# FFN tail of a gated-experts kernel: tiles taken in pairs, the grid from the absolute value in one VectorE instruction, every subtraction on VectorE, GpSimd issues the stores alone

## What is computed

```python
def _quant_e4m3(t):
    amax = jnp.max(jnp.abs(t)).astype(jnp.float32)
    scale = jnp.maximum(amax / 448.0, 1e-12)
    return (t.astype(jnp.float32) / scale).astype(jnp.float8_e4m3fn), scale

def _L0_ffn_ref(x, weight):
    w_fp8, w_scale = _quant_e4m3(weight)
    x_fp8, x_scale = _quant_e4m3(x.reshape(-1, 512))
    acc = jnp.matmul(x_fp8.astype(jnp.float32), w_fp8.T.astype(jnp.float32))
    return (acc * (x_scale * w_scale)).astype(jnp.bfloat16)

x = x + jnp.tanh(g_xattn[0]) * _L0_xattn_ref(_layernorm(x), ids, ctx, ctx, ctx)
x = x + jnp.tanh(g_ffn[0]) * _L0_ffn_ref(_layernorm(x), L0_ffn_weight)
```

## Time and profile before

| what | us |
|---|---|
| median of 3 runs | 216.4 |
| the runs | 216.09, 216.40, 217.02 |
| span of the profiled execution, first to last instruction | 215.6 |
| busy in it: VectorE | 171.0 |
| busy in it: TensorE matmul | 157.5 |
| busy in it: ScalarE | 115.8 |
| busy in it: GpSimd | 102.2 |
| tail: from the end of `x_inv` to the end of the span | 161.5 to 215.6 |

### The profile page before, as it was taken

How to read it: one execution, slowest core, us unless ns; L and a number is a source line. 1 busy time by engine, 2 the same in 40 slices (tenths; PEclk the granted TensorE clock), 3 DMA queues, 4 the chain that set the end, 5 groups by cost and what they waited for, 6 DMA issues and landing times.

```text
span 215.6 us, 3505 instructions
## 1 busy us (share of the span) xinstructions
PE 157.5 (73%) x763; PEld 76.0 (35%) x764; DVE 171.0 (79%) x377; ACT 115.8 (54%) x185; POOL 102.2 (47%) x131
## 2 busy tenths in 40 slices
PE   0224967299999999999999999996711947485710
PEld 0102343044555455545555544543200412132300
DVE  2895799898746877888778688799678999999820
ACT  2565692466546765567656633723119786536410
POOL 6177888512334323434443322156112457978671
PEclk9999999579999999999999999999665596958785
DMA  3838996000000000000000000000000002322232
GB/s 48 332 109 221 390 373 189 0 0 2 0 3 0 2 0 0 0 0 0 0 0 0 3 0 0 3 0 0 2 0 0 0 24 87 120 111 93 105 157 87
DMA packets 5643, 13.25 MB, mean 61 GB/s; under 512 B 1024, under 2 KB 1536, under 8 KB 5632
## 3 DMA queue, kind: packets, MB, share of 16 engines
q0 software_dynamic: 2560, 8.39, 11.0%
q1 hardware_dynamic: 2784, 4.73, 6.4%
q10 hardware_dynamic: 288, 0.00, 0.1%
HBM read 8.92 MB, written 4.19 MB: 61 GB/s over the span
## 4 chain that ended last, share of the span: by engine, by line
PE 43%; DVE 25%; issue 14%; POOL 8%; ACT 5%; DMA 1%; DVEq 1%; POOLq 0%
PE y_ps L448 6%; PE y_ps L440 6%; PE y_ps L453 6%; PE a_ps L448 6%; PE a_ps L440 5%; PE a_ps L453 5%; PE zT_ps L480 3%; DVE w_bits L753 3%; DVE hT_lo L1019 3%; POOL out L330 3%; POOL x L307 3%; PE hT_ps L431 3%; DVE w_lo L800 2%; DVE x L1048 1%; ACT w_hi L582 1%
## 5 line engine op out<-in xcount | busy, mean ns | idle before, releaser
L338 POOL TENSOR_TENSOR z<-az,sg 128x512 f32<-128x512 f32 x15 | 19.1, 1271 | 30.0 <-ACT az L606 21.6
L325 POOL TENSOR_TENSOR rstd<-var,minus_half 128x1 f32<-128x1 f32 x16 | 11.1, 692 | 46.5 <-DVE var L864 46.5
L604 ACT ACTIVATE sg<-a_ps,job_inv_a 128x512 f32<-128x512 f32 x19 | 13.1, 687 | 23.3 <-PE a_ps L453 19.9
L440 PE MATMUL a_ps<-w_hi,hT_hi 128*128 x76 | 22.0, 404 | 4.2 <-ACT w_hi L582 4.1
L330 POOL DMA_INDIRECT out<-x,token_of x16 | 20.1, 1254 | 8.0 <-DVE x L1048 5.1
L850 DVE SCALAR_TENSOR_TENSOR x<-y_ps,job_mul,x 128x512 f32 x19 | 14.2, 748 | 8.4 <-PE y_ps L453 8.4
L440 PE MATMUL y_ps<-w_hi,zT_hi 128*128 x76 | 19.9, 384 | 1.4 <-DVE x L850 1.4
L307 POOL DMA_INDIRECT x<-in_x,token_of x16 | 17.4, 1089 | 7.0 <-issue 4.2
L448 PE MATMUL y_ps<-w_lo,zT_hi 128*128 x76 | 20.4, 392 | 0.0
L453 PE MATMUL y_ps<-w_hi,zT_lo 128*128 x76 | 20.1, 387 | 0.0
L613 ACT ACTIVATE zT_hi<-zT_ps 128x512 f16<-128x512 f32 x19 | 11.3, 594 | 16.3 <-PE zT_ps L480 16.3
(11 more groups left out here) (161 smaller groups left out, 338.4 us busy)
## 6 DMA issues: line engine op xcount, KB each, us to landing
w<-in_ctx_t SPq DMA_DIRECT2D x4, 1024.0 KB, 9.1
wf<-in_wf_t SPq DMA_DIRECT2D x1, 512.0 KB
x<-in_x,token_of POOLq DMA_INDIRECT x16, 3.6
out<-x,token_of POOLq DMA_INDIRECT x16
g_s<-in_g_x ACTq DMA_DIRECT2D x1, 0.5 KB, 2.7
ids_s<-in_ids SPq DMA_DIRECT2D x1, 8.0 KB, 2.5
g_s<-in_g_f ACTq DMA_DIRECT2D x1, 0.5 KB, 6.5
```

Source lines behind the costliest of these rows:

```text
L338: pool.tensor_tensor(z[:, :], az[:, :], sg[:, :], ALU.mult).then_inc(z_done, 1)
L440: pe.matmul(ps, lhs_hi(k), w_block(w_hi, expert, k), start=(k == 0), stop=False)
L604: act.activation(sg[:, :], a_ps[:, :], ACT.Silu, scale=job_inv_a[:, bass.ds(j, 1)]).then_inc(silu_done, 1)
```

## The change

Only the tail's code changes, and one allocation. What it does:

- The 16 tiles form 10 groups: tiles 0 and 1 alone, six pairs (2 and 3 up to 12 and 13), tiles 14 and 15 alone. Each instruction of VectorE and ScalarE handles a group: 512 or 1024 columns. TensorE has the same transposes and matmuls, with one wait and one signal for a group.
- `scaled` takes the absolute value on ScalarE. `exponents` is gone; `grid` is vm = max(|v|, 1.5 x 2^-6) times 2^20, from |v| itself.
- `rounded` is on VectorE for all tiles, directly behind `shifted` of the same group. GpSimd has 16 stores in a row and no arithmetic.
- `finish` runs two groups behind, `scaled` four groups ahead. The four matmul results are slices of one tensor `four_ps` of four banks, and the transposes of a pair share one bank of bfloat16.
- The rings keep their sizes in tiles; ve is dropped, and `q8_done` is one counter.

The diff, without the semaphore names and the comments:

```diff
         vt = w_hi[:, :].bitcast(F32)[:, 0:NB * D].rearrange("p (b d) -> p b d", b=NB)
-        v_ve = hT_lo[:, :].bitcast(BF16).rearrange("p (b d) -> p b d", d=D)
-        v, ve = v_ve[:, 0:NB, :], v_ve[:, NB:2 * NB, :]
+        v = hT_lo[:, :].bitcast(BF16).rearrange("p (b d) -> p b d", d=D)[:, 0:NB, :]
         vm_q8 = hT_hi[:, :].bitcast(BF16).rearrange("p (b d) -> p b d", d=D)
         vm, q8 = vm_q8[:, 0:NB, :], vm_q8[:, NB:2 * NB, :]
...
+        FIRST = [0, 1, 2, 4, 6, 8, 10, 12, 14, 15, TILES]
+        GROUPS = len(FIRST) - 1
...
-        a_ps = psum("a_ps", [P, D], F32)
-        y_ps = psum("y_ps", [P, D], F32)
-        hT_ps = psum("hT_ps", [P, D], F32)
-        zT_ps = psum("zT_ps", [P, D], F32)
+        four_ps = psum("four_ps", [P, 4 * D], F32)
+        a_ps, y_ps, hT_ps, zT_ps = [four_ps[:, n * D:(n + 1) * D] for n in range(4)]
...
-        STORE_LAG = 5
-        def on_pool(i):
-            return i % 4 != 0 and i < TILES - 1
+        def tiles_of(g):
+            return range(FIRST[g], FIRST[g + 1])
+        def ring(t, g, n):
+            first = FIRST[g] % n
+            return t[:, first:first + len(tiles_of(g)), :]
+        def rows_of(t, g):
+            return t[:, FIRST[g] * D:FIRST[g + 1] * D].rearrange("p (b d) -> p b d", d=D)
+        def through(tile):
+            return next(g for g in range(GROUPS) if tile in tiles_of(g)) + 1
+        def reused(g, n):
+            last = FIRST[g + 1] - 1 - n
+            return through(last) if last >= 0 else None
...
-                pool.wait_ge(out_done, i + 1)
+                pool.wait_ge(out_done, through(i))
...
             for i in range(TILES):
-                if on_pool(i):
-                    pool.wait_ge(vt_done, i + 1)
-                    if i >= NB:
-                        pool.wait_ge(qT_done, i - NB + 1)
-                    pool.tensor_tensor(q8[:, i % NB, :], vt[:, i % NB, :], vm[:, i % NB, :], ALU.subtract)\
-                        .then_inc(q8_done[i], 1)
-                if i >= STORE_LAG:
-                    store_tile(i - STORE_LAG)
-            for i in range(TILES - STORE_LAG, TILES):
                 store_tile(i)
...
-            def transpose_q(i):
-                pe.wait_ge(q8_done[i], 1)
-                if i >= NQ:
-                    pe.wait_ge(qT_copied, i - NQ + 1)
-                for k in range(K):
-                    mm = pe.transpose(qT_ps[i % NQ][:, k * P:(k + 1) * P], q8[:, i % NB, k * P:(k + 1) * P],
-                                      ident_bf[:, :])
+            def transpose_q(g):
+                pe.wait_ge(q8_done, g + 1)
+                if g >= NQ:
+                    pe.wait_ge(qT_copied, g - NQ + 1)
+                for n, i in enumerate(tiles_of(g)):
+                    for k in range(K):
+                        mm = pe.transpose(qT_ps[g % NQ][:, n * D + k * P:n * D + (k + 1) * P],
+                                          q8[:, i % NB, k * P:(k + 1) * P], ident_bf[:, :])
                 mm.then_inc(qT_done, 1)
 
             pe.wait_ge(pool_const, 13)
             pe.wait_ge(wfq_done, K // 2)
             pe.wait_ge(wfs_done, 1 + K // 2)
             transpose_q(0)
-            for i in range(TILES):
-                if i + 1 < TILES:
-                    transpose_q(i + 1)
-                pe.wait_ge(qT_copied, i + 1)
-                if i >= NF:
-                    pe.wait_ge(y8_done, i - NF + 1)
-                for k in range(K):
-                    mm = pe.matmul(f_ps[i % NF][:, :], qT[:, i % NF, k * P:(k + 1) * P], wf_q[:, k * D:(k + 1) * D],
-                                   start=(k == 0), stop=(k == K - 1))
+            for g in range(GROUPS):
+                if g + 1 < GROUPS:
+                    transpose_q(g + 1)
+                pe.wait_ge(qT_copied, g + 1)
+                if reused(g, 4):
+                    pe.wait_ge(y8_done, reused(g, 4))
+                for i in tiles_of(g):
+                    for k in range(K):
+                        mm = pe.matmul(four_ps[:, i % 4 * D:(i % 4 + 1) * D], qT[:, i % NF, k * P:(k + 1) * P],
+                                       wf_q[:, k * D:(k + 1) * D], start=(k == 0), stop=(k == K - 1))
                 mm.then_inc(f_done, 1)
...
-            def scaled(i):
-                if i >= NB:
-                    act.wait_ge(ve_done, i - NB + 1)
-                act.activation(v[:, i % NB, :], block_of(h2, i), ACT.Copy, scale=x_inv[:, :]).then_inc(v_done, 1)
-            def copy_qT(i):
-                act.wait_ge(qT_done, i + 1)
-                if i >= NF:
-                    act.wait_ge(f_done, i - NF + 1)
-                act.activation(qT[:, i % NF, :], qT_ps[i % NQ][:, 0:D], ACT.Copy).then_inc(qT_copied, 1)
-            def to_bf16(i):
-                act.wait_ge(f_done, i + 1)
-                if i >= NB:
-                    act.wait_ge(out_done, i - NB + 1)
-                act.activation(y8[:, i % NB, :], f_ps[i % NF][:, :], ACT.Copy, scale=out_scale[:, :])\
-                    .then_inc(y8_done, 1)
+            def scaled(g):
+                if reused(g, NB):
+                    act.wait_ge(vm_done, reused(g, NB))
+                act.activation(ring(v, g, NB), rows_of(h2, g), ACT.Abs, scale=x_inv[:, :]).then_inc(v_done, 1)
+            def copy_qT(g):
+                act.wait_ge(qT_done, g + 1)
+                if reused(g, NF):
+                    act.wait_ge(f_done, reused(g, NF))
+                n = len(tiles_of(g))
+                act.activation(ring(qT, g, NF), qT_ps[g % NQ][:, 0:n * D].rearrange("p (b d) -> p b d", d=D), ACT.Copy)\
+                    .then_inc(qT_copied, 1)
+            def to_bf16(g):
+                act.wait_ge(f_done, g + 1)
+                if reused(g, NB):
+                    act.wait_ge(out_done, reused(g, NB))
+                act.activation(ring(y8, g, NB), ring(four_ps[:, :].rearrange("p (b d) -> p b d", d=D), g, 4),
+                               ACT.Copy, scale=out_scale[:, :]).then_inc(y8_done, 1)
 
             act.wait_ge(xm_step, 5)
-            V_AHEAD, Y_BEHIND = 7, 1
-            for i in range(V_AHEAD):
-                scaled(i)
-            for i in range(TILES + Y_BEHIND):
-                if i < TILES:
-                    copy_qT(i)
-                if i + V_AHEAD < TILES:
-                    scaled(i + V_AHEAD)
-                if i >= Y_BEHIND:
-                    to_bf16(i - Y_BEHIND)
+            V_AHEAD, Y_BEHIND = 4, 1
+            for g in range(V_AHEAD):
+                scaled(g)
+            for g in range(GROUPS + Y_BEHIND):
+                if g < GROUPS:
+                    copy_qT(g)
+                if g + V_AHEAD < GROUPS:
+                    scaled(g + V_AHEAD)
+                if g >= Y_BEHIND:
+                    to_bf16(g - Y_BEHIND)
...
-            def exponents(i):
-                b = i % NB
-                dve.wait_ge(v_done, i + 1)
-                if i >= NB:
-                    dve.wait_ge(vm_done, i - NB + 1)
-                dve.tensor_scalar(ve[:, b, :].bitcast(I16), v[:, b, :].bitcast(I16), EXP_MASK >> 16, None,
-                                  ALU.bitwise_and).then_inc(ve_done, 1)
-            def grid(i):
-                b = i % NB
-                dve.wait_ge(ve_done, i + 1)
-                if i >= NB:
-                    dve.wait_ge(q8_done[i - NB], 1)
-                dve.tensor_scalar(vm[:, b, :], ve[:, b, :], 2.0 ** -6, 1.5 * 2.0 ** 20, ALU.max, ALU.mult)\
+            def grid(g):
+                dve.wait_ge(v_done, g + 1)
+                if reused(g, NB):
+                    dve.wait_ge(q8_done, reused(g, NB))
+                dve.tensor_scalar(ring(vm, g, NB), ring(v, g, NB), 1.5 * 2.0 ** -6, 2.0 ** 20, ALU.max, ALU.mult)\
                     .then_inc(vm_done, 1)
 
-            def shifted(i):
-                b = i % NB
-                dve.wait_ge(vm_done, i + 1)
-                dve.scalar_tensor_tensor(out=vt[:, b, :], in0=block_of(h2, i), scalar=x_inv[:, :], in1=vm[:, b, :],
-                                         op0=ALU.mult, op1=ALU.add).then_inc(vt_done, 1)
-            def rounded(i):
-                b = i % NB
-                dve.wait_ge(vt_done, i + 1)
-                if i >= NB:
-                    dve.wait_ge(qT_done, i - NB + 1)
-                dve.tensor_tensor(q8[:, b, :], vt[:, b, :], vm[:, b, :], ALU.subtract).then_inc(q8_done[i], 1)
-            def finish(i):
-                dve.wait_ge(y8_done, i + 1)
-                dve.scalar_tensor_tensor(out=block_of(x1, i), in0=y8[:, i % NB, :], scalar=tg[:, 1:2],
-                                         in1=block_of(x1, i), op0=ALU.mult, op1=ALU.add).then_inc(out_done, 1)
-            OUT_BEHIND = 5
-            exponents(0)
+            def shifted(g):
+                dve.wait_ge(vm_done, g + 1)
+                dve.scalar_tensor_tensor(out=ring(vt, g, NB), in0=rows_of(h2, g), scalar=x_inv[:, :],
+                                         in1=ring(vm, g, NB), op0=ALU.mult, op1=ALU.add).then_inc(vt_done, 1)
```

(29 more changed lines are left out.)

4 lines of the change are left out of this document (1 added, 3 removed).

## The result

| | kernel before | changed kernel |
|---|---|---|
| median of 4 runs | 216.71 us | 211.05 us |
| the runs | 216.09 to 217.16 | 208.60 to 211.72 |
| ratio, 95% interval | | 0.971 (0.967 to 0.975) |
| span of the profiled execution | 215.6 | 210.0 |
| VectorE busy in it | 171.0 | 160.4 |

The change makes the kernel 2.9% faster by the ratio. Forecast were 211.1 us and a range of 206.8 to 214.5.

The account below looks back on a forecast made before the run. VectorE was taken to bound the tail, with stores adding the end: floor 205.5 us, plus 2.6 for half clock, 1.8 for waits at the end, 0.4 for collisions, gave span 210.3; with 0.8 around it, 211.1 us, range 206.8 to 214.5.

Parts of the forecast that it names:

- VectorE bounds, and GpSimd's subtractions cost it most: Tail: VectorE has no idle time; 11 GpSimd subtractions cost it 10.0 us, 11 stores 1.7, of 11.7 lost.
- The sum up to the last pair's finish: VectorE's tail: 31.4 us of work from 162.28 plus 0.4 for ScalarE's second \|v\|, last pair finished near 194.2.
- Waits in the middle: Finishes of pairs wait for y8 at half clock, 0.87 us more per pair; 3 of 6 pairs, 2.6 us.
- half clock throughout: Rival: TensorE at 1.2 GHz through all pairs, 5.2 us in the middle, 3.5 at the end; 216.0 us, chance 0.07.
- Waits at the end: Single groups at the end shorten VectorE's period while the last pairs' chain stays long: 1.2 to 3.5 us, taken 1.8.
- Collisions of stores with VectorE: VectorE loses 0.15 us at each of 13 stores, most of it within waits: 0.4 us, bounds 0 and 2.0.
- Behind the last pair: Stores queued after the last pair's finish: 6.55 us, then 4.76 us to the span's end.
- What lies around the tail: Tail's first VectorE instruction at 162.28 as before; 0.8 us around the span, from median 216.4 against span 215.6.
- Full clock: Rival: TensorE at 2.4 GHz through the pairs, 2.6 us goes, 1.8 becomes 1.2; span 207.1, time 207.9 us, chance 0.19.
- Stores as the bound: Rival: every store meets a pair instruction in full, 2.54 us each; 216.4 us, no change, chance 0.07.
- Table loads: Rival: ScalarE's table lacks absolute value, so switching with Copy loads tables, 1.28 us each, 14 times; 222 us, chance 0.03.
- Grid at the plain rate: Rival: VectorE's grid instruction falls to its plain rate, 6.3 us more; 217.4 us, chance 0.04.

Follow-up runs that it names:

- filler kernel: Changed kernel plus unread TensorE matmuls into a free PSUM bank before the first transposes and where TensorE would pause: 208.74 us, ratio 0.962 to the kernel before.
- second profile: Profile from timing the changed kernel, unaltered, once more on another chip: 210.01 us, ratio 0.967 to the kernel before.
- the six: Six extra GpSimd subtractions into a buffer nobody reads, one per pair, added to the changed kernel: 216.19 us, ratio 0.995 to the kernel before.

## Why the prediction was right, and where its steps were not

**VectorE bounds, and GpSimd's subtractions cost it most: right.** Forecast was 10.0 us for the subtractions and 1.7 for the stores. The experiment with only the subtractions moved measured 11.3 and 0. The step that split 11.7 us between them was wrong, by taking the 0.91 of one subtraction for all eleven; it had no effect on the sum, in which all of it went, except for the collisions below.

**Durations of pairs: right.** Forecast for grid, shifted, rounded, finish: 0.42, 1.27, 1.21, 1.27; measured 0.42, 1.28, 1.22, 1.28. Slopes taken from instructions of 512 and 2048 columns held.

**The sum up to the last pair's finish: 0.6 us short.** 37.16 us lie between the first grid (161.54) and the end of the last pair's finish (198.70); 4.61 of them are waits for y8, which leaves 32.55 for the 31.9 between 162.28 and the 194.2 of the forecast. Each of the five waits also loses the 0.08 us by which instructions overlap, 0.4. Some 0.2 is spread over shifted and rounded.

**Waits in the middle: right mechanism, sized by luck.** 2.6 forecast; 0.34 + 1.82 + 0.48 + 1.19 = 3.8 measured in the first profile and 0.34 + 0.35 + 0.63 = 1.3 in the second. That the chain fits at full clock was right for pairs (no wait at three finishes in the filler kernel). Two terms were missing or mis-sized. A pair at half clock between pairs at full clock waits for most or all of the 1.7 us between chain and period (1.82 and 1.19 us measured), not for the 0.87 that was worked out for half clock throughout. And the first finish (0.34, at half clock) and the first pair's at full clock (0.35 and 0.36) wait where VectorE's period is shorter beside single tiles, which had no term. The even share of half and full clock was about right for the first profile (2 of 6 pairs at half clock and one mixed) and not for the second (one mixed). The finish three behind took all of these waits away.

**Waits at the end: too large.** 1.8 forecast, 0.78 measured on the path (0.80 in the second profile), with the last stretch at full clock throughout; at full clock throughout the forecast had 1.2. The 0.26 after it lies beside a queued store. The sign "over 0.5 us a group at full clock" is met only here, where the prediction itself had waits.

**Collisions of stores with VectorE: none.** 0.4 forecast (bounds 0 and 2.0), 0 measured. Stores are the ones that wait.

**Behind the last pair: right.** 6.55 forecast, 6.47 measured, then 4.83 against 4.76.

**What lies around the tail: two errors that cancel.** The tail began 0.74 us sooner than in the profile of before; the instruction that writes `x_inv` starts between 160.4 and 161.4 us in the profiles of all kernels here, and the changed code is not ahead of it. What lies around the span is 1.7 us (211.72 for the profiled run, span 210.0), not 0.8: the median of before was set against the span of a different execution, and that gave too little. And the profiled run lies 0.7 above the median. Term by term, span: 210.3 forecast, less 0.74, plus 0.6, plus 1.2, less 1.0, less 0.4 makes 210.0, as measured. The hit within 0.1 us is luck in part; errors of up to 1.2 us stood in its terms, and with the waits of the second profile the middle would have been 1.3 too long instead.

**The rivals.** Full clock: made with fillers, a span of 206.7 for 207.1. Stores as the bound: 1283 ns in the mean, far from 2.54 us. Table loads: there is one in the whole profile, as before, so the absolute value is in the loaded table. Grid at the plain rate: 418 to 420 ns for a pair. Half clock throughout did not occur, and wasn't tried.

## What to carry to other kernels

When two engines work side by side on the same memory, look at the mean length of the busier one's instructions before counting what the other one relieves it of: here 11 subtractions, worth 6.6 us on VectorE, cost it 11.3 on GpSimd. Larger instructions save a fixed part each (3 us of VectorE's time here), but make the pipeline coarser; waits for results ate the gain here until the consumer was moved one group further behind. And look at the ends apart from the middle: a distance that frees the middle queues work at the end, where smaller groups and shorter distances are better.

## What the runs showed of the hardware

A VectorE instruction that meets a GpSimd subtraction stands still until 0.2 us before its end (184.40 and 184.59). The subtraction waits in the same way for a VectorE instruction that is under way when it starts. The first of the six, with the VectorE instruction beside it:

```profile
167.73 2.19 POOL L399 TENSOR_TENSOR spare<-w,wf_m 128x512 bf16<-128x512 f32 x1 [10.19 <-DVE w_hi L1040]
```

```profile
167.69 1.22 DVE L1048 TENSOR_TENSOR hT_hi<-w_hi,hT_hi 128x1024 bf16<-128x1024 f32 x1
```

It ends at 169.92, 1.01 us behind the VectorE instruction (168.91), and so do three of the other five. In the remaining two VectorE came out of a wait for y8 while GpSimd issued a store (182.42 to 183.39), and the finish recorded from 182.81 on stood behind a subtraction recorded from 183.42 on; GpSimd's records are rough. The Trainium skill, SBUF — State Buffer, section "SBUF: two separate sides", has the lock for a whole instruction, held by whoever starts first. The trace agrees in four of the six cases (1.01 us); in these two it does not, if the starts are taken as recorded.

The prediction cites the same section of the Trainium skill, SBUF — State Buffer, for starved stores. Its box on them speaks of VectorE's two-port modes. Here stores also wait for VectorE's instructions with two tensor inputs, and a subtraction on VectorE holds one up as a finish does. In the second profile of the changed kernel:

```profile
195.17 1.44 POOL L342 DMA_INDIRECT out<-x,token_of  x1 [1.41 <-DVE x L1041]
```

```profile
195.07 0.69 DVE L1037 TENSOR_TENSOR hT_hi<-w_hi,hT_hi 128x512 bf16<-128x512 f32 x1
```

The store ends 0.85 us behind the subtraction (195.76) and takes 1.44 us for 0.98 alone.

Stores issued by GpSimd lengthen nothing on VectorE, but can themselves wait through more than one of its instructions. In the experiment with pairs and kept exponents one store took 3.06 us:

```profile
185.54 3.06 POOL L343 DMA_INDIRECT out<-x,token_of  x1 [1.14 <-DVE x L1048]
```

```profile
184.99 1.28 DVE L1036 SCALAR_TENSOR_TENSOR w_hi<-w,x_inv,hT_hi 128x1024 f32<-128x1024 f32 x1
186.19 0.42 DVE L1030 TENSOR_SCALAR hT_hi<-hT_lo 128x1024 bf16<-128x1024 bf16 x1
186.52 1.22 DVE L1044 TENSOR_TENSOR hT_hi<-w_hi,hT_hi 128x1024 bf16<-128x1024 f32 x1
187.66 1.28 DVE L1048 SCALAR_TENSOR_TENSOR x<-y,tg,x 128x1024 f32<-128x1024 bf16 x1
```

It ends at 188.60, 0.86 after the third of these (187.74). With only the subtractions moved, stores took 1.72 us each in the middle and ended 0.85 after the second instruction; one took 2.58 through three. In the changed kernel, where `rounded` waits for the end of `shifted` and leaves 0.03 us between them, none waited for more than one. That this gap is what lets a store in was not tested, and it can't be all: the store from 194.54 ended at 196.10, 0.85 behind the finish at its start (195.25), though VectorE's next instruction had started at 195.17. The prediction's worst price of a store, 2.54 us, assumed one instruction; it is no upper bound.
